# Second attention's queries and keys by Strassen's method in column chunks, with the graph branch placed anew

## The reference, cut to what matters

```python
# graph branch (GATv2, 4 heads of 64), over the 10625 edges (src, dst) and one more loop for each node
xl, xr = (x @ W_down @ Wl), (x @ W_down @ Wr)            # x scaled by its root mean square
e = sum(leaky_relu(xl[src] + xr[dst], 0.2) * att)        # one logit for each edge and head
alpha = softmax of e over the edges that share dst
out_graph = segment_sum(alpha * xl[src], dst) @ W_up

# attention branch (Performer, 16 heads of 64, 266 random features)
q, k, v = x @ Wq, x @ Wk, x @ Wv
qp = ratio * (exp(dash_q - diag_q - max over features) + eps)
kp = ratio * (exp(dash_k - diag_k - max over nodes and features) + eps)
out_mix = (qp @ (kp.T @ v)) / (qp @ kp.sum(nodes)) @ Wo + bo
```

## Time and profile before

| what | value |
|---|---|
| median of three runs | 1730.36 us |
| the profiled execution | 1727.01 us |
| its span (first to last instruction) | 1724.7 us |
| PE busy | 1677.6 us, 97% of the span |
| DVE busy | 832.8 us, 48% |
| POOL busy | 657.1 us, 38% |
| ACT busy | 413.8 us, 24% |

### The profile page before, as it was taken

The page is one execution under the profiler, slowest core; times in us unless marked ns, Lnnn a source line. Parts: engine busy times, 40 slices in busy tenths (PEclk is TensorE's granted clock), DMA queues, the critical chain, the costliest instruction groups (busy, mean ns, idle before and its releaser), DMA issues. The chain is left out here.

```text
span 1724.7 us, 21026 instructions
## 1 busy us (share of the span) xinstructions
PE 1677.6 (97%) x7904; PEld 1044.4 (61%) x7904; DVE 832.8 (48%) x1643; ACT 413.8 (24%) x770; POOL 657.1 (38%) x537
## 2 busy tenths in 40 slices
PE   9999999999999999999999999998998999999998
PEld 6466446444444677755477775556676766776633
DVE  5887344562722332245455554867653223222337
ACT  1000000001411101110277772752111222122232
POOL 0565886220000057777788872000031322222213
PEclk9999999999999999999899999999999999999999
DMA  9655115453450043333322222724075999999951
GB/s 349 214 146 152 2 1 139 121 183 70 168 210 5 0 127 108 97 98 100 89 54 57 54 53 59 178 93 161 0 215 183 399 410 401 412 416 414 397 140 60
DMA packets 103755, 281.70 MB, mean 163 GB/s; under 512 B 61745, under 2 KB 69155, under 8 KB 91282
## 3 DMA queue, kind: packets, MB, share of 16 engines
q1 hardware_dynamic: 28755, 218.54, 34.3%
q0 software_dynamic: 67872, 50.79, 13.3%
q10 hardware_dynamic: 7052, 11.35, 2.1%
HBM read 250.37 MB, written 29.80 MB: 162 GB/s over the span
## 5 line engine op out<-in xcount | busy, mean ns | idle before, releaser
L1015 POOL DMA_INDIRECT table_d<-wring x85 | 178.2, 2097 | 108.3 <-issue 67.9
L1409 POOL DMA_INDIRECT wring<-xl_d,wring x85 | 109.5, 1288 | 254.4 <-DMA xr_d<-flat_b 228.5
L1422 POOL DMA_INDIRECT score_d<-wring x85 | 111.2, 1308 | 72.0 <-DMA score_d<-wring 45.1
L469 PE MATMUL bank<-flat_d,wring 128*128 128x312 f32 (+1 forms) x512 | 135.0, 426 | 0.0
L3007 PEld LDWEIGHTS bank<-picked_flat,wring 128*128 128x128 f32 x1152 | 129.4, 192 | 7.7 <-issue 7.7
L3007 PE MATMUL bank<-picked_flat,wring 128*128 128x128 f32 x1152 | 131.3, 276 | 0.0
L469 PEld LDWEIGHTS bank<-flat_d,wring 128*128 128x128 f32 x512 | 96.8, 189 | 37.9
L1409 POOL DMA_INDIRECT wring<-xr_d,wring x85 | 109.8, 1291 | 25.9 <-issue 23.8
L3014 PE MATMUL bank<-wring,picked_flat 128*64 128x256 f32 x640 | 75.0, 388 | 4.4 <-PEq L2480 4.4
L3119 PE MATMUL bank<-wring,region_a 128*125 128x512 f32 x160 | 70.6, 604 | 2.7 <-issue 2.7
L1696 PE MATMUL bank<-wring,flat_d 128*125 128x512 f32 x160 | 71.5, 599 | 0.8 <-ACT flat_c L2224 0.5
(11 more groups left out here) (484 smaller groups left out, 2978.8 us busy)
## 6 DMA issues: line engine op xcount, KB each, us to landing
wring<-in_experts SPq DMA_DIRECT2D x57, 2048.0 KB, 19.9
wring<-in_L_Ws SPq DMA_DIRECT2D x6, 2048.0 KB, 17.0
table_d<-eq_buf SPq DMA_DIRECT2D x2, 3072.0 KB, 28.0
score_d<-no_edge SPq DMA_DIRECT2D x2, 3072.0 KB, 32.7
wring<-table_d POOLq DMA_DIRECT2D x10, 610.4 KB, 7.3
wring<-score_d SPq DMA_DIRECT2D x5, 1093.8 KB
wring<-pid_d ACTq DMA_DIRECT2D x17, 312.5 KB
wring<-in_edge_w ACTq DMA_DIRECT2D x17, 312.5 KB
```

The source lines that it names most:

```text
L469: ins = pe.matmul(bank[:, 0:n], w[:, k * HALF + m * P:k * HALF + (m + 1) * P], act_t[:, k, at:at + n], start=(k == 0), stop=(k == chunks - 1))
L1015: pool.indirect_dma_start(out=tables_d[b % 2], out_offset=bass.IndirectOffsetOnAxis(ap=edge_at[:, b:b + 1], axis=0), in_=edge_sums[:, b, : ...
L1409: pool.indirect_dma_start(out=to[:, g % 2, j, :], out_offset=None, in_=table, in_offset=bass.IndirectOffsetOnAxis(ap=index[:, b:b + 1], ax ...
L1422: pool.indirect_dma_start(out=score_d, out_offset=bass.IndirectOffsetOnAxis(ap=cell_i[:, b:b + 1], axis=0), in_=logit[:, b, :], in_offset= ...
```

## The change

1. `pe_gemm_cols` for queries and keys is replaced by two calls of `pe_gemm_columns`, with sums of the tokens kept in free parts of flat_b, of the ring and of one new buffer that holds kf, qf and qf_t later. s3 and s1 are made before the down product's last piece is copied, s2 and s4 after xl and xr.
2. The right half of Wk is loaded in two parts by columns, since its slot holds Wq's left half, which the new scheme needs to its end: the first part once chunk 1 of the queries is done with it.
3. The order of the products in a first chunk is p1, p7, p6, p2, p5, p4, p3 where the sums of the tokens exist already (keys, Ws3). The wait for the last column c12 of the product before moves from ahead of p1 to ahead of p5; one for c21 stands ahead of p7.
4. Edge groups 0 to 3 are worked on beside queries and keys, one DVE step behind a named Strassen step. Groups 4 to 7 come after value tiles 0, 2, 4 and 6. The late groups start at earlier units.
5. The graph softmax's turn, rows and up products stand one output tile earlier.
6. Two memsets of v1 move from POOL to DVE, behind the keys.

```diff
@@ Weights.issue
+            if n in self.in_parts:
+                first_free, first_in = self.in_parts[n]
+                sp.wait_ge(*first_free)
+                self.load_columns(sp, slot, src, 0, first_in[0])
                 sp.wait_ge(*self.freed[last])
+            if n in self.in_parts:
+                self.load_columns(sp, slot, src, HALF // 2, self.loaded[slot])
...
+    def load_columns(self, sp, slot, src, at, done):
+        to, of = (x.rearrange("p (k c) -> p k c", c=HALF)[:, :, at:at + HALF // 2]
+                  for x in (self.ring[:, slot, :], src))
+        sp.dma_start(to, of).then_inc(done, 16)
@@ tensor engine
-                pe_gemm_cols(pe, x1_t, ring=sring, beside=ends)
-                pe_gemm_cols(pe, x1_t, ring=sring)
+                pe_gemm_columns(pe, x1_t, queries2_cols, x1_sums, free_queries, ends)
+                wt.in_parts[K2_LOADS[1]] = ((queries2_cols.filled, queries2_cols.fills["p4", 1]), (columns_in, 48))
+                pe_gemm_columns(pe, x1_t, keys2_cols, x1_sums, free_keys, last=queries2_cols)
...
-                pe_gemm_columns(pe, x3_t, ws3_cols, col_sums, units_free)
+                pe_gemm_columns(pe, x3_t, ws3_cols, col_sums, units_free, last=ws1_cols)
@@ placement
-        QK_GROUPS = 5
-        V_GROUP_AT = {1: 5, 3: 6, 6: 7}
+        QK_GROUPS = 4
+        V_GROUP_AT = {0: 4, 2: 5, 4: 6, 6: 7}
+        EARLY_STEPS = (("q", 0, "u3"), ("q", 0, "c21"), ("q", 1, "t2"), ("q", 1, "t1"),
+                       ("q", 2, "t2"), ("q", 2, "t1"), ("q", 2, "u3"), ("q", 2, "c21"),
+                       ("q", 3, "t2"), ("q", 3, "t1"), ("q", 3, "u3"), ("q", 3, "c21"),
+                       ("k", 0, "u3"), ("k", 0, "c21"), ("k", 1, "t2"), ("k", 1, "t1"),
+                       ("k", 2, "u3"), ("k", 2, "c21"), ("k", 3, "t2"), ("k", 3, "t1"))
-        LATE_STARTS = (0, 9, 19, 30, 41, 52, 63, 74)
-        LAST_START = 83
+        LATE_STARTS = (0, 7, 16, 27, 38, 48, 59, 69)
+        LAST_START = 80
-        TURN_AT = {5: 0, 6: 1, 7: 2, 8: 3, 9: 4}
-        ROWS_AT = {6: 0, 7: 1, 8: 2, 9: 3}
+        TURN_AT = {4: 0, 5: 1, 6: 2, 7: 3, 8: 4}
+        ROWS_AT = {5: 0, 6: 1, 7: 2, 8: 3, 9: 4}
-        UP_AT = {7: 0, 8: 1, 9: 2}
+        UP_AT = {6: 0, 7: 1, 8: 2, 9: 3}
@@ vector engine
+                def beside_queries(i, name):
+                    if (i, name) == (0, "first_t3"):
+                        root_mean_squares()
+                    if (i, name) == (0, "t2"):
+                        graph_rows()
+                        dve_token_sums(v, x1_t, queries2_cols, x1_sums, ("s2", "s4"))
+                        edge_cells()
+                    if ("q", i, name) in EARLY_STEPS:
+                        next(early)
...
+                for _ in early:
+                    pass
+                v.memset(v1[:, :, :, DH:DH + 1], 1.0).then_inc(features_set, 1)
+                v.memset(v1_flat[:, T * HEADS * (DH + 1):], 0.0).then_inc(features_set, 1)
@@ scalar engine
-                for buf in (q1_t, k1_t):
-                    for m, cols, bank in cols_tiles(s, ring=sring):
-                        s.activation(buf[:, m, cols], bank, ACT.Copy, scale=DN).then_inc(s_emptied, 1)
+                for f, to in ((queries2_cols, q1_t), (keys2_cols, k1_t)):
+                    for i in range(4):
+                        s.wait_ge(f.filled, f.fills["p1", i])
+                        s.activation(to[:, 4 + i, 0:HALF_N], banks[CX][:, 0:HALF_N], ACT.Copy, scale=DN)\
+                            .then_inc(f.copied, 1)
+                        s.wait_ge(f.filled, f.fills["p2", i])
+                        s.activation(to[:, i, 0:HALF_N], banks[CX][:, 0:HALF_N], ACT.Copy, scale=DN)\
+                            .then_inc(f.copied, 1)
```

More of the change, by code:

```diff
@@ L211, in __init__ @@
                 self.steps[name, i + 1 if name == "t3" else i] = n_steps
+                if (name, i) == ("t2", 0):
+                    for late in late_sums:
+                        n_steps += 1
+                        self.steps[late, 0] = n_steps
             for name in copies:
@@ L680, in gps_kernel, with pe_gemm_columns @@
         CX, CY, CZ, CW = 4, 5, 6, 7
-        def pe_gemm_columns(pe, x, f, sums, free_x, after_product=None):
-            left, right = wt.take(pe), None
+        def pe_gemm_columns(pe, x, f, sums, free_x, after_product=None, last=None):
+            left, right, right_load = wt.take(pe), None, wt.taken
             def product(name, i, bank, w, k0, moving, add=False):
@@ L716, in pe_gemm_columns @@
                             until("c21", i - 1)
-                        else:
-                            right = wt.take(pe)
+                        elif last:
+                            pe.wait_ge(last.stepped, last.steps["c21", 3])
+                        if i == 0:
+                            right = wt.take(pe, first=True)
+                        if i == 2:
+                            wt.wait_loaded(pe, right_load)
                         product("p7", i, CZ, right, 0, summed(0))
@@ L721, in pe_gemm_columns @@
                         until("t2", i)
+                        if i == 0 and ("s2", 0) in f.steps:
+                            until("s2", i)
                         product("p6", i, CY, left, 0, summed(1))
@@ L756, in dve_gemm_columns, with add @@
             left, right = (wt.slot_of[n] for n in loads)
-            wt.wait_loaded(v, loads[1])
+            wt.wait_loaded(v, loads[1], first=True)
+            def add(out, bank, before):
+                if scale:
+                    v.scalar_tensor_tensor(out=out, in0=bank, scalar=scale, in1=before, op0=ALU.mult, op1=ALU.add)\
+                        .then_inc(f.stepped, 1)
+                else:
+                    v.tensor_tensor(out, bank, before, ALU.add).then_inc(f.stepped, 1)
             for i in range(4):
@@ L783, in dve_gemm_columns @@
                 v.wait_ge(f.stepped, f.steps["u3", i])
[L784 removed]
+                add(u3(i), banks[CW][:, 1:HALF_N], u3(i))
                 beside(i, "c22")
@@ new lines, in graph_rows, with edge_cells @@
+                def graph_rows():
+                    for t in range(T):
+                        v.tensor_scalar(xlr[:, t, :], dring.consume(v)[0:R, :], rstd[:, t:t + 1], None, ALU.mult)\
+                            .then_inc(d_emptied, 1)
+                    xlr_made.append(dring.taken)
+                def edge_cells():
+                    v.wait_ge(gat_in, 48)
+                    gat_step.mark(v.tensor_copy(src1_f, src1_i))
+                    gat_step.mark(v.tensor_copy(dst1_f, dst1_i))
+                    after(v, gat_step)
+                    gat_step.mark(v.scalar_tensor_tensor(out=src1_f, in0=dst1_f, scalar=float(N), in1=src1_f,
+                                                         op0=ALU.mult, op1=ALU.add))
+                    after(v, gat_step)
+                    v.tensor_copy(cell_i[:, 0:EB], src1_f).then_inc(cells_made, 1)
```

190 lines of the change are left out of this document (111 added, 79 removed).

## The result

The changed kernel takes **1737.36 us**, the median of 8 runs (1734.63 to 1741.26); the kernel before takes 1729.12 (8 runs, 1726.36 to 1730.54). The ratio is **1.0049**, 95% interval [1.0037, 1.0061]: slower by 8.2 us, where I had forecast 1725 and a gain. The profiled execution took 1737.41 us, with a span of 1735.3.

What follows compares the result with a forecast made beforehand. PE, busy 97%, was taken to bound the kernel, with POOL's gather chain limiting attention's lead. 1727.0 - 4.3 - 0.5 + 2.1 - 0.6 = 1723.7 us, or 1727.1 from the runs' median; forecast 1725, range 1716 to 1731.

Steps and rivals of the forecast that it cites:

- Q and K, -16.7: Queries and keys: 448 records instead of 512, eight chunks in 118.2 us instead of 134.9, so -16.7 us.
- The wait of p4 in the queries: Chunk 0 of the queries: p4 follows p5 directly and waits for DVE's t4, +1.3 us.
- Group 2's gather, 2 us taken of 0 to 6: Keys' chunk 0: group 2's last gather lands late and stalls PE at p4, 0 to 6 us, 2 taken.
- I take 0.6 us more delay than before: POOL's scatters behind weight loads: 0.6 us more delay, bounds 0 to 9, leaving POOL a 6.0 us lead at block 54.
- POOL's lead at block 54 (group 10): Attention's narrow place: POOL's gathers there come 6.0 us earlier than before, and attention cannot lead by more.
- DVE waits at unit 16, 7 us; attention -4.3: Attention: DVE waits 7 us for group 10's gather; lead 6.0 less 1.7 lost to the clock ends attention 4.3 earlier.
- I estimate 4.3 + 7 us: Graph softmax: score table earlier by 4.3 + 7 us, so the first maximum comes 17 us into the output product.
- where I had -0.5: Output product and softmax: waits for ACT unchanged in sum, but 0.48 us ahead of the last up product goes, -0.5.
- The boundary +2.1, Ws3 -0.6: Block's end: DVE's norms end 2.1 us behind PE, +2.1; Ws3: waits go, -1.8, but p7 needs t3, +1.2, so -0.6.
- The first rival: POOL does not bind: gathers come 7 us earlier than reckoned, all 12.9 us of lead arrives, 1715.1 us; chance 0.2.
- The second: Softmax late: first maximum stays 24 us behind the output product's start, 6.5 more than the sum, 1730.2 us; chance 0.15.
- the third: Each pair of loads holds a scatter for both, 9 us: POOL's lead -2.4, attention 4.1 later, 1732.1 us; chance 0.15.

Runs made afterwards that it cites:

- e6: The changed kernel without the gathers of xr (xl is added to itself): 1712.66 us, ratio 0.9910 to the kernel before.
- e7: The kernel before without the gathers of xr (xl is added to itself): 1728.46 us, ratio 1.0000 to the kernel before.
- e2_late: The changed kernel with the late edge groups back at the units of before: 1738.50 us, ratio 1.0051 to the kernel before.
- e19_apart: The changed kernel with its two back-to-back pairs of weight loads taken apart: 1733.69 us, ratio 1.0027 to the kernel before.
- e13_pieces: The changed kernel with large weight loads issued in pieces, each after the one before has landed: 1721.56 us, ratio 0.9958 to the kernel before.
- e9_oneinput: The changed kernel with each edge group's leaky relu and product with att replaced by one-input reductions of equal length: 1754.09 us, ratio 1.0151.

## Why the prediction was wrong

- *Q and K, -16.7.* Right: from 592.90 to 728.73 are 135.8 us with two stalls; without them and the slow clock behind the second, and less the 8.7 us of xl and xr, it is 118.6 (118.2 forecast). e6 against e7 gives 15.8 for the whole change. The wait of p4 in the queries was 0.98 (1.3).
- *Group 2's gather, 2 us taken of 0 to 6.* 5.14 us, and 2.5 more because the clock fell behind it, which I had left out. The last gather was forecast to issue at 662.4 and issued at 666.66: the DMAs ahead of it had already lasted 5.9 us over 1.21 each, where before it was 1.5. It landed 8.7 us later, just behind my bound of 675. With the loads in pieces the stall is 1.17.
- *"I take 0.6 us more delay than before".* **This step failed.** POOL's lead at block 54 (group 10) was forecast as 6.0; it was -1.8. Waits for landings took 2.9 of the lost 8.4, between my 0.6 and my bound of 9. The larger part, 5.8 up to that gather, is a term that I did not have: DMAs that POOL starts under a two-input operation of DVE. The rows of before showed it (a gather of 2.18 us at 701.26, under the add of group 3), and I had used 1.53 us for every DMA. DVE and POOL before:

```profile
700.85 1.49 DVE L1451 TENSOR_TENSOR wring<-wring 125x1280 f32<-125x1280 f32 x1 [16.19 <-DMA wring<-xr_d,wring]
```

```profile
701.26 2.18 POOL L1409 DMA_INDIRECT wring<-xr_d,wring  x1 [0.30 <-issue]
```

- *DVE waits at unit 16, 7 us; attention -4.3.* It waits 4.27 us there and 3.25 at unit 7; the output product begins 0.4 us later than before. Lead of POOL, not of PE, sets it, as argued. But e2_late shows that the earlier starts were not needed: at the old units the lead survives the attention.
- *"I estimate 4.3 + 7 us" for the score table.* **Failed too**, the costliest step. The first maximum came 26.7 us into the output product instead of 17, and from that product's start to the boundary's first transpose PE took 123.7 us instead of 113.2: less the boundary's 1.7 this is +8.8, where I had -0.5. The wait of 6.15 us for group 15's logits went, as said, but I took all of it as time won. The last eleven scatters go one per landing, 2.8 us apart or more, whoever made them wait: 5.5 us late at the last gather, POOL was still 2.8 late at the last scatter. Nor was it lateness alone: with pieces, where POOL is early, the first maximum still comes 23.6 us into the product, close to the 24.0 of before, and PE waits 2.23 and 3.72 us. So the step one tile earlier rested on a gain that isn't there.
- *The boundary +2.1, Ws3 -0.6.* 1.7 and -0.8: right.

The first rival, that POOL doesn't bind, fell. The rivals were priced one at a time. The second (softmax late, +6.5) and the third (POOL's lead at -2.4, 1732.1) hang on one chain, POOL's, and came together: 1738.6, where 1737.4 was measured. That is close in part by luck: the loss split otherwise, with attention 0.4 us later instead of 4.1 and the softmax 8.8 instead of 6. The range ended at 1731 because their chances were taken as apart. The third's mechanism, pairs of loads, was wrong (e19_apart); its number was met by single loads and the longer DMAs. The page that I cited for it (the Trainium skill, DMA: Bandwidth & Descriptors, "Queues, rings and completion order": a completion is counted only behind the engine's earlier writes) agrees with e13_pieces, where 0.25 MB ahead of a scatter holds it no longer.

## What to carry to other kernels

When PE gets faster, look for the chain that no engine's busy share shows: here 255 small DMAs on an engine that is busy for 38%, of which every third, a scatter, waits until the scatter before it has landed. Price every term that hangs on it from one lead, not as independent rivals. A large load that shares the DMA engines with small latency-bound ones goes in pieces, each after the landing of the one before; here that cost nothing, since the data wasn't needed soon, and it gained only where the small ones bound.

## What the runs showed of the hardware

- A DMA that POOL starts while DVE runs an operation with two inputs in SBUF takes as much longer as that operation still runs, less 0.12 us: 0.79 for 0.92, 1.18 for 1.29. Of the 74 DMAs that start with over 0.3 us of it left (before, changed kernel, e9_oneinput), 72 follow this within 0.04. Taking the second input away in two of the three such steps of each edge group took the excess from 30.9 to 15.6 us. The Trainium skill (SBUF — State Buffer, "Who interferes with whom") tells of a probe in which tensor_tensor stalled no DMA, and infers that it leaves alone the port that the generation of descriptors needs; these indirect DMAs it did hold up.
- A piece of 0.25 MB that waits for the landing of the one before takes 2.8 us at W_up (22.7 us for eight, 833.0 to 855.7), against 4.5 us between two scatters.
